# A fused eight-block transformer kernel on one core: SyncE's queue order in the last stage, and later loads for every other group of differential attention

## The reference, cut to what matters

```python
# differential attention: two score maps per head, mixed, and a second softmax
scores = softmax(energy / sqrt(D))                  # (b, 2, h, q, k), causal
diff = softmax(where(causal, NEG, scores[:, 0] - lam * scores[:, 1]))
att = einsum('bhqv,bvhd->bqhd', diff, v)
...
# scan over 64 chunks of 16 tokens, state S of 16x16 per head
kh = k_i @ S;  v_new = f(kh, v_i - k_i);  qh = q_i @ S - tril(q_i k_i^T * eta) @ v_new
o = q_i + LN(qh);  S = S - (k_i * eta)^T @ v_new
# then gate, normalise, project, add, and the gated network on the result
```

## Time and profile before

| | |
|---|---|
| median of 3 runs | 3016.36 us (3016.28 to 3024.55) |
| profiled execution | 3036.48 us, span 3034.7 us |
| differential attention | about 1253 to 2035 us of the span |
| last stage | about 2358 to 3034 us |
| projections in the last stage | until about 2585 us |

### The profile page before, as it was taken

One profiled execution on the slowest core, in us unless ns is written; L12 is line 12 of the kernel. 1 busy time (PEld: TensorE's weight loads), 2 busy tenths in 40 slices (PEclk: granted clock), 3 DMA queues, 4 the chain that ended last, 5 costly groups with the idle time before them and its releaser, 6 DMA issues. The chain is left out here.

```text
span 3034.7 us, 68702 instructions
## 1 busy us (share of the span) xinstructions
PE 2472.5 (81%) x25105; PEld 1658.0 (55%) x25192; DVE 2081.4 (69%) x4873; ACT 1836.1 (61%) x3580; POOL 897.9 (30%) x971
## 2 busy tenths in 40 slices
PE   7888868888888698777676677768999686899998
PEld 3433326643333384444344444447888465788988
DVE  5488886677777567799898899974333344666652
ACT  2588964315445443599788898973222333667778
POOL 2233324111111322455455555530000222223223
PEclk9979988969999798899999999988999767899999
DMA  4533302243432113601222022004000656622210
GB/s 158 150 70 69 69 3 100 83 105 57 57 45 26 72 59 109 115 11 20 30 29 28 3 29 29 2 6 167 1 1 1 146 100 99 132 37 32 33 43 8
DMA packets 283034, 177.09 MB, mean 58 GB/s; under 512 B 205649, under 2 KB 242529, under 8 KB 280673
## 3 DMA queue, kind: packets, MB, share of 16 engines
q1 hardware_dynamic: 273552, 164.55, 26.0%
q10 hardware_dynamic: 9168, 8.41, 1.2%
HBM read 113.84 MB, written 54.66 MB: 56 GB/s over the span
## 5 line engine op out<-in xcount | busy, mean ns | idle before, releaser
L1364 ACT ACTIVATE ad_e<-ps,ad_nm 128x1024 f32<-128x1024 f32 (+7 forms) x512 | 383.5, 756 | 81.0 <-DVE ad_nm L1425 78.4
L1425 DVE TENSOR_REDUCE ad_nm<-ps 128x1 f32<-128x1024 f32 (+7 forms) x512 | 369.4, 748 | 36.6 <-PE ps L1293 35.8
L1398 POOL TENSOR_TENSOR ad_e<-ad_e,ad_c 128x128 f32<-128x128 f32 (+7 forms) x256 | 293.3, 1146 | 16.5 <-DVE ad_rz L1438 10.1
L663 ACT ACTIVATE ab_e<-ps 128x512 f32<-128x512 f32 (+3 forms) x384 | 167.1, 491 | 190.6 <-PE ps L578 189.4
L1291 PE MATMUL ps<-fd_k_st,fd_q_st 96*128 96x512 bf16 (+3 forms) x768 | 214.4, 340 | 70.2 <-ACT ad_e L1364 52.0
L388 PE MATMUL ps<-warm,ident_b 128*128 128x512 bf16 x425 | 139.1, 393 | 114.6 <-ACT ad_prT L1349 112.5
L1449 DVE CUSTOM_DVE_ANT_0 ad_t<-ad_e,ad_rz 128x128 f32<-128x128 f32 (+7 forms) x256 | 223.3, 872 | 4.2 <-ACT ad_pr L1372 2.4
L1391 POOL TENSOR_TENSOR ad_e<-ad_e,later_k 128x128 f32<-128x128 f32 x256 | 118.8, 464 | 355.4 <-ACT ad_e L1364 355.4
L1372 ACT ACTIVATE ad_pr<-ad_t,ad_low 128x128 f32<-128x128 f32 (+7 forms) x256 | 200.1, 782 | 0.0
L1306 PE MATMUL ps<-ident,ad_pr 128*128 128x128 f32 x1152 | 175.8, 281 | 24.0 <-ACT ad_pr L1372 24.0
L1910 POOL TENSOR_TENSOR st_it_low<-st_it,st_it_high 128x256 fp32r<-128x256 f32 x128 | 98.5, 782 | 316.9 <-ACT st_it_high L2173 311.5
(11 more groups left out here) (389 smaller groups left out, 7119.3 us busy)
## 6 DMA issues: line engine op xcount, KB each, us to landing
scr_a<-pa_parts SPq DMA_DIRECT2D x24, 512.0 KB, 2.8
fa_q_st<-scr_a SPq DMA_DIRECT2D x24, 512.0 KB, 7.9
split<-f_split SPq DMA_DIRECT2D x16, 768.0 KB, 3.9
fd_q_st<-scr_d SPq DMA_DIRECT2D x48, 256.0 KB, 8.0
g_w<-split SPq DMA_DIRECT2D x8, 1536.0 KB, 18.0
scr_d<-pd_parts SPq DMA_DIRECT2D x20, 384.0 KB, 2.7
st_w_first<-split ACTq DMA_DIRECT2D x5, 1536.0 KB, 7.3
fa_k_st<-scr_a SPq DMA_DIRECT2D x24, 256.0 KB, 8.6
```

The costliest lines, as they stand in the source:

```text
L663: act.activation(e[:, u % ER, h, lo:QB], m.ps[:, n4(u, h) % 3, lo:QB], ACT.Exp, scale=scale).then_inc(s_read[0], 1)
L1364: act.activation(e[:, u % EB, s, 0:L], src, ACT.Exp, bias=nm[:, u % EB, s:s + 1], accum_out=z[:, u % EB, s:s + 1]).then_inc(exped[s], 1)
L1398: pool.tensor_tensor(e[:, k, 1, 0:L], e[:, k, 1, 0:L], c[:, k:k + 1].to_broadcast([P, L]), ALU.mult).then_inc(mixed, 1)
L1425: dve.tensor_reduce(nm[:, u % EB, s:s + 1], src, AX.X, ALU.max, negate=True).then_inc(maxed[s], 1)
```

## The change

The differential attention's loads of groups 3, 5 and 7 wait for three more rows of the group before them (`DELAY`). In the last stage SyncE's queue gets another order: `relay` is split into `relay_out` and `relay_in`, and `keep(4)` and `keep(7)` move between the halves, ahead of the octet loads; the waits for `kept[3]` to `kept[6]` stand later; the loads of `w_late` move ahead of the second octet load. The eight transfers that load `y` become one of 256 KB. On ScalarE the first `rows` are issued ahead of the first `straight`, and `load_weights` moves from lag 2 to lag 11, so slots 11, 14, 17, 20 and 23.

```diff
-    EB = 4
+    EB, DELAY = 4, 3
...
-                    sp.wait_ge(valued, BT * (g - 1))
+                    sp.wait_ge(valued, BT * (g - 1) + (DELAY if g % 2 else 0))
...
-            def relay(j):
+            def relay_out(j):
                 n = slice(j * OCT, (j + 1) * OCT)
                 sp.wait_ge(qh_copied, (j + 1) * OCT)
                 for h in range(HL):
                     sp.dma_start(a["scr_q"][:, n, :, head(h)], tb[head(h), n, :, 0:CH]).then_inc(y_out, 16)
+
+            def relay_in(j):
+                n = slice(j * OCT, (j + 1) * OCT)
                 if j >= 2:
                     sp.wait_ge(o_gained, 3 * (j - 1))
                 for k in range(2):
                     sp.dma_start(base_gain[:, j % 2, k], a["scr_o"][k, j]).then_inc(bg_in, 16)
                 sp.wait_ge(y_out, 16 * HL * (j + 1))
-                for k in range(OCT):
-                    sp.dma_start(y[k * CH:(k + 1) * CH, j % 2], a["scr_q"][:, j * OCT + k, :, :]).then_inc(y_in, 16)
+                sp.dma_start(y[:, j % 2].rearrange("p g x -> p (g x)"),
+                             a["scr_q"][:, n, :, :].rearrange("t n g x -> n t (g x)")).then_inc(y_in, 16)
...
             keep(sp, 3)
-            was_kept(sp, 3)
-            relay(0)
+            relay_out(0)
+            keep(sp, 4)
+            relay_in(0)
             next_octet(0)
-            keep(sp, 4)
-            was_kept(sp, 4)
             keep(sp, 5)
-            was_kept(sp, 5)
+            for j in (3, 4, 5):
+                was_kept(sp, j)
             rows(sp, 2)
             keep(sp, 6)
-            was_kept(sp, 6)
-            relay(1)
-            next_octet(1)
+            relay_out(1)
             keep(sp, 7)
+            relay_in(1)
             was_kept(sp, 7)
             for c in range(FIRST, MLP // C):
                 sp.dma_start(weights(c).bitcast(F32), a["split"][c]).then_inc(w_in[c], 16)
+            next_octet(1)
+            was_kept(sp, 6)
             rows(sp, 3)
             for j in range(2, NBLK):
-                relay(j)
+                relay_out(j)
+                relay_in(j)
...
-                act.wait_ge(y_in, 16 * OCT * (j + 1))
+                act.wait_ge(y_in, 16 * (j + 1))
...
                     was_kept(act, 0)
+                    rows(act, 0)
                     straight(act, 0)
-                    rows(act, 0)
...
-                           (2, load_weights)], NCH)
+                           (PRE + 1, load_weights)], NCH)
```

## The result

The changed kernel takes 3010.11 us (median of ten runs), the kernel before, run between them, 3021.11 (3016.28 to 3032.64). One run of the ten was in a slow state, twice as long, and is left out of everything but that median: the other nine lie between 2995.05 and 3014.36. It is not the ratio of the two medians, which lie 11 us apart; the two differ by up to 3 us in the experiments too, and where a gain is given in us it comes from the ratio. Measured again at the end of the study the same kernel gave 0.9944 (0.9921 to 0.9966). So it is faster, by about half of the 25.8 us that I forecast, and outside my range of 2979 to 3005.

The account below looks back on a forecast made before the run. No engine bounds the whole span; stalls at attention's loop jump and behind SyncE's queue in the last stage cost time. Terms -14.5 - 11.3 - 3 + 3 = -25.8 us took the median 3016.4 to 2990.6, range 2979 to 3005.

Parts of the forecast that it names:

- The direction: Whole kernel: the change makes it faster, given 0.92, against 0.05 for the same and 0.03 for slower.
- The jump (-14.5): Differential attention, slot 14 of groups 2 and 4: gaps of 8.58 and 8.16 us shrink to 1.12 each, gaining 14.5 us.
- rival A: Differential attention: the gap moves along with the loads or is the jump's own, so attention gives nothing; 3005 us, 8%.
- The bounds of 13.8 to 17.0: Differential attention: limits in us on the gain at both jumps, from group 2's length against groups 3 and 6.
- The delayed loads (0): Differential attention: issuing the odd groups' loads three rows later costs nothing by itself, 0 us.
- The cover of 23 us: Differential attention, group 3: delayed loads are in place 50 us after the boundary, first score at 73 without the gap.
- `keep(4)` (-11.3): Last stage: storing it ahead of the octet load removes ScalarE's 14.14 us wait before `p_sigmoids(6)`, gaining 11.3 us.
- `w_late` and `rows(3)` (-3): Last stage: `w_late` earlier and `rows(3)` behind the octet load gain between 0 and 6.5 us, taken as 3.
- The 6.5 us that I hoped to cut: Last stage: the slot with `rows(3)` behind three weight tiles takes 13.65 us against 7.16 an octet later.
- Weight tiles at later slots (+3): Last stage: tiles moved to slots 20 and 23 meet other loads, losing 0 to 9.1 us, taken as 3.
- One transfer, the swap and the waits (0): Last stage: `y` as one transfer and `rows` swapped with `straight` give 0; no wait over 1 us in the new order.
- Rival B: Last stage gives back its gain: weight tiles cost 9.1 us (2999.7), or `keep(4)`'s place only uncovers `keep(5)` (3001.9); 12%.

## Why the prediction was right and wrong

**The direction** was right, and so were the places that the profile named. **The size** was wrong, by the price of the jump and by the edits of the last stage that the sum took to cancel each other.

*The jump (-14.5).* Wrong in size, and the first step that failed. "Less twice the 1.12 us that a jump costs in quiet" took the price of another loop's jump; here the quiet jump has 3.79 us of gap, and with the slow clock behind it 4.6 us of time. The row copies of the kernels that keep all loops and have the delay take 745.9 us in the mean of eleven executions, those without it 754.8 (four): 8.9 us. The mechanism (a fetch of the loop's first instructions, held up by the loads) is borne out by the transfers of instructions, and rival A, "or is the jump's own", held for half of the gap. That more than one engine fetches at once I didn't see, since only the last one shows. The bounds of 13.8 to 17.0 were no bounds: they came from the lengths of groups without a jump, and so left out that a jump stays.

*The delayed loads (0).* Right as far as it can be seen. The cover of 23 us held, and no one waited for the data. The three steps that are 1.38 us longer in this execution are stretches of the lower clock, the third with no load in flight; in other executions with the same loads they are absent or elsewhere, and the kernels without the delay have them too.

*`keep(4)` (-11.3).* Right: 23.66 to 12.17 us in every kernel that has only this edit in the queue, 11.5 us. Alone it gave 14 us in the time.

*`w_late` and `rows(3)` (-3).* Wrong in sign, and the second step that failed. "The same bytes still have to be moved, only earlier and in another order" took for granted that a storm is never worse for another place. In the whole change TensorE loses 4.8 us in the step behind `w_late`, in both of its profiled executions, and 3.8 to 6.7 in the four others that have that order of SyncE's queue with the early waits. The 6.5 us that I hoped to cut come and go: that step takes 13.65 us in the profiled execution before, 7.93 after, 8.81 in the kernel before run again.

*Weight tiles at later slots (+3).* Not seen: the move alone gave 0.9931 against 0.9919, its return 0.9957 against 0.9953, both no difference, and the move alone adds no step to its trace. By the intervals 3 us can't be ruled out. The gap of 4.55 us that I priced it by the earlier trace rows stands in the changed kernel too (4.58 us), whose first tile goes out at the same slot 11; no run parts the tile from the octet load there.

*One transfer, the swap and the waits (0).* Each alone 0.9932 and 0.9938 against 0.9919, none to be told from it. What share of the give-back is theirs is open.

*The sum.* -8.9 and -11.5 are 20.4; the two edits measure 24.5 (18 to 31). The rest of the change was priced at 0 (-3 and +3) and costs about 10, with the wide interval given above, which gives the 14 measured. Rival B, the last stage gives back what it gains, is thus what happened, together with half of A; I had them at 12 and 8%, each by itself. But B came by another way than the ones I named: the weight tiles cost nothing that can be seen, and a storm of `w_late` that cost "what it did" would have cost nothing new. That A and B could come together was left out of the range, which so ended 5 us too early.

*What stays open*: how the give-back in chunk copies 10 to 22 is shared between the edits, why TensorE's longer code costs 7 to 10 us in the same stretch, and why the clock falls less often where the loop is written out.

## What to carry to other kernels

A gap "for issue" at the first instruction of a loop's body is the jump, and it can stand on several engines at once, hidden behind the one that comes last (here TensorE and VectorE at least): price what stays of it from the same loop in quiet, not from another one, and try the loop written out on all engines. Moving transfers away from it buys half. The profile's transfers of instructions tell whether such a gap is a fetch, and how long the fetch was held up.

A store that waits in a queue behind loads, and has a reader with a deadline, is worth moving by itself; measure that one line before more is reordered. The reorderings around it, costed at nothing together, took back some 10 of 25 us.

When single executions of a kernel differ by 10 us, take the durations between fixed marks in several of them, and believe only the steps that repeat. Where a step is longer without a wait, look at its granted clock before blaming what runs beside it.

## Of the hardware, what I had not expected

- A jump of this loop costs 3.4 to 4.0 us of idle TensorE in quiet and 7.6 to 8.6 with 13 loads in flight; straight code at the same place, with a DMA share of 0.7, nothing.
- In the jump's gap the transfer that brings TensorE's code starts 5.4 us after the gap under the loads' backlog and within 0.9 us of it in quiet.
- With TensorE's loop gone, VectorE had its own gap of 6.7 and 7.4 us there.
- Straight code can be late too: in the last stage TensorE has gaps for issue of 2.87 and 4.58 us without a jump, the first with a transfer of its code inside it and a DMA share near 1.
- The granted clock falls to its lower level (0.50) around a jump's gap of 3.8 us, with a mean of 0.61 over the 6 us behind it, and stays at 1.00 throughout the step where there is none. It also fell for 3.4 us where TensorE had been busy 7.83 of 11.7 us.
- 319 GB/s beside the last stage's small matmuls cost 0.7 us in one kernel and 288 GB/s 4.9 in another, where `w_late` had gone out 6.5 us ahead of the step.
